# Two expert tiles' inner values side by side: three TensorE turns a double step in place of four, in a fused attention and mixture-of-experts kernel

## The reference, cut to what matters

```python
B, S, D, E, F, FS = (4, 256, 256, 64, 176, 352)      # TOP_K = 6
scores = jax.nn.softmax(x @ gate_w.T, axis=-1)
topk_w, topk_idx = jax.lax.top_k(scores, TOP_K)
...
g = jnp.einsum('ecd,efd->ecf', buf, w_gate)
u = jnp.einsum('ecd,efd->ecf', buf, w_up)
eo = jnp.einsum('ecf,edf->ecd', jax.nn.silu(g) * u, w_down)
gathered = eo[se, pos_c] * (sw * valid.astype(sw.dtype))[:, None]
```

## Time and profile before

| | before |
|---|---|
| median of 3 runs | 1659.45 us (1658.81 to 1660.39) |
| the profiled execution | 1659.82 us |
| its span, first to last instruction | 1658.0 us |
| TensorE (PE) busy | 1496.2 us, 90% |
| VectorE (DVE) busy | 1272.3 us, 77% |
| ScalarE (ACT) busy | 1003.2 us, 61% |
| GpSimd (POOL) busy | 786.5 us, 47% |
| `phase_experts` from the first turn of rows to the last scatter | 936 to 1513 us of the span |

### The profile page before, as it was taken

How to read it: one execution, slowest core, us unless ns; L and a number is a source line. 1 busy time by engine, 2 the same in 40 slices (tenths; PEclk the granted TensorE clock), 3 DMA queues, 4 the chain that set the end, 5 groups by cost and what they waited for, 6 DMA issues and landing times. The chain is left out here.

```text
span 1658.0 us, 44404 instructions
## 1 busy us (share of the span) xinstructions
PE 1496.2 (90%) x12590; PEld 1005.8 (61%) x12655; DVE 1272.3 (77%) x4402; ACT 1003.2 (61%) x2284; POOL 786.5 (47%) x848
## 2 busy tenths in 40 slices
PE   7995889999999999999974499999999999997997
PEld 4664667677777777777763255555555555554775
DVE  4663777888888888889884587777777777773887
ACT  4773676767667776676661266666666666662221
POOL 1333233666666666666677334433433443442333
PEclk9996899999999999999995699999999999998999
DMA  3874454554555542223223666666666667524996
GB/s 115 258 236 154 128 156 124 158 160 150 156 160 160 159 148 89 88 82 94 92 69 108 175 183 203 195 194 199 201 192 195 205 191 204 183 79 97 251 246 144
DMA packets 264982, 264.40 MB, mean 159 GB/s; under 512 B 87467, under 2 KB 236313, under 8 KB 264752
## 3 DMA queue, kind: packets, MB, share of 16 engines
q1 hardware_dynamic: 203504, 175.70, 36.8%
q0 software_dynamic: 19968, 51.16, 8.5%
q10 hardware_dynamic: 41280, 34.77, 8.3%
HBM read 142.70 MB, written 122.98 MB: 160 GB/s over the span
## 5 line engine op out<-in xcount | busy, mean ns | idle before, releaser
L1745 POOL DMA_INDIRECT scratch_y<-e_eo,e_goes x224 | 222.6, 994 | 357.8 <-ACT e_eo L1828 314.4
L1770 PE MATMUL e_psGU<-wexp,e_xT 128*64 x896 | 290.1, 467 | 0.0
L1772 PE MATMUL e_psGU<-e_up,e_xT 128*64 128x352 f32 x896 | 290.0, 467 | 0.0
L1374 POOL TENSOR_TENSOR f_wnr<-f_wss,f_half 128x4 f32<-128x4 f32 x96 | 112.2, 1169 | 197.0 <-DVE f_wss L1197 196.9
L1364 POOL DMA_INDIRECT scratch_buf<-rows,dest x180 | 183.2, 1018 | 44.9 <-issue 43.5
L1849 ACT ACTIVATE e_up<-wexp 128x704 f32 x224 | 176.9, 790 | 20.6 <-POOLq L1735 20.6
L1770 PEld LDWEIGHTS e_psGU<-wexp,e_xT 128*64 128x64 f32 x896 | 113.8, 137 | 121.8 <-issue 121.8
L1964 DVE COPY e_down<-wexp 128x512 f32 x224 | 94.1, 420 | 101.2 <-PE e_psD L1793 99.2
L1828 ACT ACTIVATE e_eo<-e_psD 128x256 f32<-128x256 f32 x224 | 85.7, 385 | 93.7 <-PE e_psD L1793 47.0
L1817 ACT ACTIVATE e_sgm<-e_psGU 128x176 f32<-128x176 f32 x224 | 71.2, 318 | 93.3 <-PE e_psGU L1772 92.1
L1787 PE MATMUL e_psD<-wexp,e_hT 112*64 x448 | 115.2, 378 | 1.6 <-DVE e_hT L1925 1.6
(11 more groups left out here) (332 smaller groups left out, 4365.2 us busy)
## 6 DMA issues: line engine op xcount, KB each, us to landing
e_xg<-scratch_buf ACTq DMA_DIRECT2D x448, 66.0 KB
scratch_y<-f_blank SPq DMA_DIRECT2D x64, 384.0 KB
c_g<-scratch_y SPq DMA_DIRECT2D x64, 384.0 KB, 5.8
scratch_qkvT<-q_tT SPq DMA_DIRECT2D x16, 768.0 KB
wexp<-in_wgT SPq DMA_DIRECT2D x64, 176.0 KB
wexp<-in_wuT SPq DMA_DIRECT2D x64, 176.0 KB
scratch_buf<-f_blank SPq DMA_DIRECT2D x65, 132.0 KB, 1.9
scratch_kv<-q_y SPq DMA_DIRECT2D x16, 512.0 KB, 2.8
```

Source lines behind the costliest of these rows:

```text
L1374: pool.tensor_tensor(wnr[:, x, cols], wss[:, x, cols], half[:, 0:Q], ALU.pow).then_inc(wn1[x].sem, 1)
L1745: pool.indirect_dma_start(out=T["y"], out_offset=bass.IndirectOffsetOnAxis(goes[:, n:n + 1], 0), in_=eo[:, n % OB, :], in_offset=None, bou ...
L1770: pe.matmul(psGU[0:RT, n % 2, 0:2 * F], xT[:, n % 4, k, 0:RT], ring[:, bass.ds(at[n] + k * 2 * F, 2 * F)], start=(k == 0), stop=(k == KD - 1))
L1772: mm = pe.matmul(psGU[RT:P, n % 2, 0:2 * F], xT[:, n % 4, k, RT:P], up2[:, n % 2, k * 2 * F:(k + 1) * 2 * F], start=(k == 0), stop=(k == K ...
```

## The change

The even tile's 176 inner values and the odd tile's last 64 are laid next to each other in `hh`, so that the two tiles' last 64 make one block of 128 columns. One turn of this block gives both: the even tile's 64 come to lie on partitions 0 to 63 and the odd tile's on 64 to 127, where `down_rest` reads them already. The odd tile's own 112 follow behind them, so its product is written in two pieces (64 and 112 wide) in place of one of 176. The copy of the even tile's turned values is 128 wide in place of 256.

```diff
-        hh = sb("hh", [P, 2, FM + P])
+        hh = sb("hh", [P, 2 * F + P - FM])
...
             def turn_h(n):
                 pe.wait_ge(hd, thru(n))
                 pe.wait_ge(htd, thru(n - 2))
-                lo = FM if n % 2 == 0 else F - P
-                pe.transpose(psH[:, n % 2, 0:P], hh[:, n % 2, 0:P], ident[:, :])
-                pe.transpose(psH[:, n % 2, P:2 * P], hh[:, n % 2, lo:lo + P], ident[:, :]).then_inc(hp, 1)
+                if n % 2 == 0:
+                    pe.transpose(psH[:, 0, 0:P], hh[:, 0:P], ident[:, :]).then_inc(hp, 1)
+                else:
+                    pe.transpose(psH[:, 1, 0:P], hh[:, 2 * F - FM:2 * F + P - FM], ident[:, :])
+                    pe.transpose(psH[:, 1, P:2 * P], hh[:, FM:2 * F - FM], ident[:, :]).then_inc(hp, 1)
...
-                pe.matmul(psD[0:RT, n % 2, 0:D], hT[rows, n % 2, 1, 0:RT], rest[rows, :], start=False, stop=True)
-                pe.matmul(psD[RT:P, n % 2, 0:D], hT[rows, n % 2, 1, RT:P], down2[rows, n % 2, D:2 * D], start=False, stop=True).then_inc(dp, 1)
+                pe.matmul(psD[0:RT, n % 2, 0:D], hT[rows, 1, 1, 0:RT], rest[rows, :], start=False, stop=True)
+                pe.matmul(psD[RT:P, n % 2, 0:D], hT[rows, 1, 1, RT:P], down2[rows, n % 2, D:2 * D], start=False, stop=True).then_inc(dp, 1)
...
-                v.tensor_copy(hT[:, n % 2, :, :].rearrange("p k t -> p (k t)"), psH[:, n % 2, 0:2 * P]).then_inc(htd, 1)
+                if n % 2 == 0:
+                    v.tensor_copy(hT[:, 0, 0, :], psH[:, 0, 0:P]).then_inc(htd, 1)
+                else:
+                    v.tensor_copy(hT[:, 1, :, :].rearrange("p k t -> p (k t)"), psH[:, 1, 0:2 * P]).then_inc(htd, 1)
...
-                v.wait_ge(hp, thru(n - 2))
-                v.tensor_tensor(hh[:, n % 2, 0:F], psGU[:, n % 2, F:2 * F], sgm[:, n % 2, :], ALU.mult).then_inc(hd, 1)
+                v.wait_ge(hp, thru(n - 1 - n % 2))
+                if n % 2 == 0:
+                    v.tensor_tensor(hh[:, 0:F], psGU[:, 0, F:2 * F], sgm[:, 0, :], ALU.mult).then_inc(hd, 1)
+                else:
+                    v.tensor_tensor(hh[:, F:2 * F - FM], psGU[:, 1, F + FM:2 * F], sgm[:, 1, FM:F], ALU.mult)
+                    v.tensor_tensor(hh[:, 2 * F - FM:2 * F], psGU[:, 1, F:F + FM], sgm[:, 1, 0:FM], ALU.mult).then_inc(hd, 1)
```

More of the change, by code:

```diff
@@ L1965, in keep_down @@
                 v.tensor_copy(rest[rows, :], ring[rows, bass.ds(first + D, D)]).then_inc(down_kept, 1)
-            v.memset(hh[:, 0, F:FM + P], 0.0)
+            v.memset(hh[:, 2 * F:2 * F + P - FM], 0.0)
             v.wait_ge(rank_d, 1)
```

## The result

| | before | after |
|---|---|---|
| median | 1659.82 us, 4 runs (1658.81 to 1660.39) | 1646.24 us, 4 runs (1645.94 to 1646.89) |
| profiled execution, its span | 1659.82, 1658.0 us | 1645.94, 1644.2 us |

The ratio is 0.9924, with a 95% interval of 0.9909 to 0.9939: the changed kernel is faster by 13.6 us, where 12.2 was forecast (1646.24 against 1647.3). The two medians give 0.9918, inside the interval. The profiled spans differ by 13.8 us.

The account below looks back on a forecast made before the run. TensorE was taken to bound the expert phase: 110 double steps at 0.110 us give 12.1 us, with 0.13 for the last even copy 12.2, so 1659.45 - 12.2 = 1647.3 us. Range 1645.8 to 1650.5 us.

Parts of the forecast that it names:

- What bounds the kernel: In the expert phase TensorE is full, 482.00 of 482.00 us; the other engines wait for it.
- The price, 0.110 us a turn: Each turn left out on TensorE saves the distance between starts, 0.110 us, over 110 double steps 12.1 us.
- The split product, +0.08: VectorE's odd product in two pieces takes 0.08 us more per double step, at most 0.34, hidden by its waits.
- The margin: From the odd product's end to its turn's weight load: 1.07 us, 0.96 after the change, enough to cover the split.
- The loader (rival 2): Expert loading is the true limit and takes the gain back: no change, 1659.4 us; chance 0.04.
- the new waits: `hidden(n)` waits for the previous tile's turns, the even `down_rest` for the odd copy; both claimed to cost nothing.
- The last even copy, 0.13 once: In the last double step TensorE waits for the turned values' copy; 128 columns fewer save 0.13 us, once.
- The sum: 12.1 us from TensorE's double steps and 0.13 from the last even copy, together 12.2 us off the total.
- after the phase everything starts 12.2 us earlier: Phases are separated by barriers, so what follows the expert phase moves forward by 12.2 us; profiled span 1645.8 us.
- Rival 3: VectorE's second odd piece is held until the first is through, so the odd turn waits: 14 us slower, 1673; chance 0.03.

Follow-up runs that it names:

- turn_put_back: The changed kernel with the even tile's second turn put back, its values unused; undisturbed double step 5.00 us.
- split_alone: The kernel before with only the odd tile's product split into two pieces; undisturbed double step 5.00 us.
- copy_of_before: The kernel before, unedited, rerun where it takes 1702 us; 563.23 us from first `gate_up` to last turn, undisturbed double step 5.00 us.
- copy_of_after: The changed kernel, unedited, rerun where the kernel before takes 1702 us; median 1696.72 us, undisturbed double step 4.89 us.

## Why the prediction was right

- **What bounds the kernel.** Right. TensorE is full in both traces, and the gain is the number of steps by the turn's distance.
- **The price, 0.110 us a turn.** Right: 0.109 over 106 steps, and 0.11 again from four to three to two turns. By the lone product's 56 ns of the Trainium skill ("TensorE: Matmul & The Clock Gate", "Back-to-back issue gap") the step would have been 4.94; the trace has 4.89. The same page's 107 ns for a load of 128 columns (LDWEIGHTS) is near the 109 of the trace.
- **The split product, +0.08.** The pieces are 0.224 and 0.264 us (forecast 0.23 and 0.28), and together 0.40, so the addition is 0.06 where I took 0.08. Their durations sum to 0.15 more than the single product's 0.34; the overlap takes back the rest. The median margin fell from 1.36 to 1.18, by 0.18: 0.11 for the earlier turn and 0.06 for the pieces, to the rounding of the rows.
- **The margin.** Right in its conclusion for this run, no TensorE wait for `e_hh` but 0.7 us at the phase's start. My 1.07 us came from one step that was late, and the median is 0.2 more (1.36 against 1.18 there, both to the turn's start). But I took it for a property of the program. It is one of ScalarE's pace in that run: the copies have 0.48, and a third of the steps have none.
- **The loader (rival 2), the new waits.** Covered, as forecast; VectorE's wait for `down_rest` fell from 0.92 to 90.5/107 = 0.85 a step, within the 0.05 to 0.3.
- **The last even copy, 0.13 once.** Wrong, and tiny: from the last turn to the last `down` it is 1505.78 - 1503.91 = 1.87 before and 1492.47 - 1490.63 = 1.84 after, 0.03 less.
- **The sum.** The term of the double steps was 12.1 and measured 12.1 from the first `turn_x` to the last turn, the total 13.6. That the term fits so closely is in part luck: I left out the last double step, which gained its 0.11 too, and 0.59 us lost in the first one are made up by 0.56 gained just ahead of it. The step that was off is "after the phase everything starts 12.2 us earlier", which let all other stretches be equal: 1.2 us came ahead of the phase and 0.5 behind it. The spans of single runs of one kernel differ by 0.5 us (1644.2 to 1644.7 after), and I have no run that would make more of these pieces than scatter.
- **Rival 3**, slower through the odd product: not in this run, but a late odd product does hold TensorE elsewhere. No run shows one piece held by the other, as rival 3 had it; the lateness is ScalarE's. In the second set the changed kernel has 28 long steps and the one before 16, and 3.8 of the 11.6 us are given back. That the change's own use of margin does this is likely and not shown: each count is of one execution, and turn_put_back and split_alone, which undo or keep only a part, lie between (5.8 and 6.0 us of excess). Its threshold of 1.07 us was not tried where the kernel takes 1659 us; in the other set, with a median margin of 0.40 us, half a microsecond was already beyond the margin.

## What to carry to other kernels

Where one engine is full and the trace shows a stretch without the removed instruction, its price is the distance between starts, not the duration, and the count of steps gives the sum. The cover of what is added is worth reading as a distribution over all steps, not at one: a margin of another engine's product belongs to that engine's pace, and should be quoted with what ends the idle time of the engine ahead of it. Such a margin lies on a round through several engines, and an engine with little slack on that round, here ScalarE, can use it up where another run of the same program shows none of it.

## What the runs showed of the hardware

The same program took 1659 us in one set of runs and 1702 in the other, with equal granted clock (0.958 in the profiled executions of the kernel before and its copy) and with undisturbed double steps equal to 0.01 us. Most of the 43 us lie ahead of the phase, whose first `turn_x` is 36 us later in copy_of_before than before, and 46 in copy_of_after than after. Inside it `silu(n+1)` is held on ScalarE behind its own issue of a row load, mostly for 1.0 to 1.2 us, in 37 of 93 double steps of copy_of_before and in none of the first pair. The row loads' issues (0.49 us) and the register loads (0.31 us) are as long in both sets, so neither is slower by itself. Moving the register loads makes the held steps fewer (31 of 95 to 21 of 98 in the changed kernel, 81 of 87 to 32 of 95 with two more products). What holds ScalarE, and why only in one set, has no cause that the runs name.
